# A GAT layer's neighbour differences: made on GpSimd into three buffers instead of on VectorE

## What is computed

```python
h = (x @ W).reshape(G, Jn, H, C)
es = einsum('gjhc,hc->gjh', h, a_s)[:, src]
ed = einsum('gjhc,hc->gjh', h, a_d)[:, dst]
e = leaky_relu(es + ed, 0.2)
alpha = softmax of e over the edges that end in dst
out = zeros.at[:, dst].add(alpha[..., None] * h[:, src]) + bias
x = gelu(layer_norm(out + x @ R, g, b))
```

## Time and profile before

| | us |
|---|---|
| median of 3 runs | 4858.85 (4856.44 to 4862.07) |
| the profiled execution | 4847.68 |
| its span | 4845.9 |
| TensorE busy | 4262.9 (88% of the span) |
| VectorE busy | 3549.6 (73%) |
| ScalarE busy | 2615.6 (54%) |
| GpSimd busy | 627.6 (13%) |
| share of the chain that ended last: TensorE, VectorE, ScalarE, GpSimd | 64%, 18%, 7%, 1% |

### The profile page before, as it was taken

The page is one execution under the profiler, slowest core; times in us unless marked ns, Lnnn a source line. Parts: engine busy times, 40 slices in busy tenths (PEclk is TensorE's granted clock), DMA queues, the critical chain, the costliest instruction groups (busy, mean ns, idle before and its releaser), DMA issues.

```text
span 4845.9 us, 72897 instructions
## 1 busy us (share of the span) xinstructions
PE 4262.9 (88%) x22774; PEld 1939.4 (40%) x22774; DVE 3549.6 (73%) x8027; ACT 2615.6 (54%) x3930; POOL 627.6 (13%) x746
## 2 busy tenths in 40 slices
PE   4687989898998988989988898988899898899988
PEld 4223343443434334343433434344343433434345
DVE  1577777877778877777887777787777887777762
ACT  0454655556565555655555565555555555565643
POOL 1111201111020111102011120111102011110100
PEclk9898999999999999999999999999999999999998
DMA  2000000000000000000000000000000000000000
GB/s 95 2 1 3 1 3 4 2 5 1 3 4 4 4 2 5 1 3 4 3 4 1 6 1 3 4 3 4 1 4 3 4 4 2 5 1 4 3 2 6
DMA packets 23087, 25.64 MB, mean 5 GB/s; under 512 B 3395, under 2 KB 21835, under 8 KB 22139
## 3 DMA queue, kind: packets, MB, share of 16 engines
q1 hardware_dynamic: 22650, 20.26, 1.3%
HBM read 16.06 MB, written 4.19 MB: 4 GB/s over the span
## 4 chain that ended last, share of the span: by engine, by line
PE 64%; DVE 18%; issue 8%; ACT 7%; POOL 1%; DVEq 0%; SPq 0%; DMA 0%; ACTq 0%; POOLq 0%
PE bank L859 11%; PE bank L812 8%; PE bank L925 7%; PE bank L916 6%; PE bank L696 5%; PE bank L829 4%; PE bank L770 3%; PE bank L850 2%; PE bank L815 2%; ACT X L1264 2%; PE bank L708 2%; DVE X L1870 2%; DVE Ho L2019 2%; PE bank L832 1%; PE bank L846 1%
## 5 line engine op out<-in xcount | busy, mean ns | idle before, releaser
L1870 DVE TENSOR_TENSOR X<-X,bank 128x1024 f32<-128x1024 f32 (+2 forms) x432 | 483.7, 1140 | 268.2 <-PE bank L736 153.2
L1264 ACT ACTIVATE X<-X,c_vec 128x1024 f32<-128x1024 f32 (+2 forms) x432 | 498.3, 1176 | 298.3 <-DVE X L1870 297.2
L1308 ACT ACTIVATE X<-bank,bgc 128x512 f32<-128x512 f32 (+1 forms) x624 | 419.2, 672 | 441.9 <-PE bank L859 441.9
L916 PE MATMUL bank<-XT,c_w 128*128 128x512 f32 x1024 | 509.6, 626 | 28.6 <-ACT SQ L1344 26.6
L925 PEld LDWEIGHTS bank<-c_w,SQ 128*128 128x128 f32 x4096 | 481.9, 192 | 56.5 <-issue 50.2
L925 PE MATMUL bank<-c_w,SQ 128*128 128x128 f32 x4096 | 500.8, 277 | 0.0
L812 PE MATMUL bank<-R,c_W 64*128 64x512 f32 (+1 forms) x832 | 473.3, 650 | 28.4 <-issue 23.3
L532 POOL TENSOR_TENSOR R<-X 128x512 f32<-128x512 f32 (+1 forms) x208 | 257.3, 1241 | 1613.4 <-PE bank L812 838.5
L859 PE MATMUL bank<-R,c_C 128*128 128x512 f32 (+1 forms) x832 | 460.2, 635 | 0.0
L846 PE MATMUL bank<-X,WR 64*128 64x512 f32 (+1 forms) x832 | 455.9, 637 | 0.0
L1344 ACT ACTIVATE SQ<-bank,c_vec 128x512 f32<-128x512 f32 x512 | 345.4, 686 | 164.6 <-PE bank L916 162.5
(11 more groups left out here) (258 smaller groups left out, 6822.5 us busy)
## 6 DMA issues: line engine op xcount, KB each, us to landing
c_w<-in_w SPq DMA_DIRECT2D x2, 2048.0 KB
out<-Ho SPq DMA_DIRECT2D x32, 128.0 KB, 2.6
c_fpW<-in_fpW SPq DMA_DIRECT2D x1, 3200.0 KB
X<-in_x SPq DMA_DIRECT2D x34, 75.0 KB, 1.9
X<-in_txt SPq DMA_DIRECT2D x32, 64.0 KB, 1.8
X<-in_chain SPq DMA_DIRECT2D x1, 1300.0 KB
X<-in_sel SPq DMA_DIRECT2D x1, 600.0 KB
X<-in_sel SPq DMA_DIRECT2D x1, 300.0 KB
```

What stands on the lines that cost most here:

```text
L916: mm(hidden_bank(e, m), w1[:, k * P:k * P + P], XT2[:], start=True, stop=True).then_inc(hid_ps, 1)
L1264: A_(dst, dst, ACT.Gelu, bias=v(f"b{l}"), scale=v(f"g{l}")).then_inc(x_ok, 1)
L1308: A_(dst, bZ[k % 2][:, 0:cols], ACT.Identity, bias=bias).then_inc(zs_ok, 1)
L1870: TT(dst, dst, b, ALU.mult).then_inc(u_ok, 1)
```

## The change

`neighbours` of layer 2 loses its difference (two VectorE instructions, one link semaphore and two waits for each chunk) and reads a finished D. A new function `differences_2` on GpSimd makes it, with the same two instructions, into three new buffers `DH` that take the place of the slices of `DR`. It stands in GpSimd's order behind `edges_0` of the next pass and ahead of `pose_pads`. For chunk c it waits for h of chunk c+1 and for VectorE's result of chunk c-2 (which read the buffer). VectorE waits for the new semaphore `dh_ok`; ScalarE's copy of chunk n waits for `dh_ok` of difference n-3, where it waited for VectorE's whole chunk n-3. The constant `LINKS` follows the 13 links that are gone.

```diff
+        DH = [R[:, k * NCOL:(k + 1) * NCOL] for k in (2, 3, 5)]
...
+            def differences_2(s):
+
+                a0 = T0[2] - NT0
+                for c in range(NCH):
+                    n, last_c = joints(c) * P, c == NCH - 1
+                    pool.wait_ge(d_sb, s * AGG + a0 + min(c + 2, NCH))
+                    pool.wait_ge(t_ok, s * AGG + a0 + max(c - 1, 0) + 1)
+                    d, h = DH[c % 3], HS[c % 3]
+                    if last_c:
+                        before_memset(0)
+                        nc.gpsimd.memset(d[:, n - P:n], 0.0)
+                    else:
+                        TT(d[:, n - P:n], HS[(c + 1) % 3][:, 0:P], h[:, n - P:n], ALU.subtract)
+                    TT(d[:, 0:n - P], h[:, P:n], h[:, 0:n - P], ALU.subtract).then_inc(dh_ok, 1)
...
                     edges_0(s + 1)
+                differences_2(s)
+                if nxt:
                     pool.wait_ge(z_ps, s * TASKS + T0[2] + 9)
                     pose_pads(s + 1)
...
-                        act.wait_ge(t_ok, s * AGG + k - 1)
+                        act.wait_ge(dh_ok, s * NCH + n - 2)
...
-            LINKS, LINKS_ANY = 213, 123
+            LINKS, LINKS_ANY = 200, 123
...
                 if l == 2:
-                    dve.wait_ge(t_ok, s * AGG + k + 1)
-                    dve.wait_ge(d_sb, s * AGG + a0 + min(n + 2, NCH))
-                    d, h = DR[:, 0, c % 2, :], HS[c % 3]
-                    if c + 1 < NCH:
-                        TT(d[:, cols - P:cols], HS[(c + 1) % 3][:, 0:P], h[:, cols - P:cols], ALU.subtract)
-                    else:
-                        nc.vector.memset(d[:, cols - P:cols], 0.0)
-                    link(TT(d[:, 0:cols - P], h[:, P:cols], h[:, 0:cols - P], ALU.subtract))
+                    d, before = DH[c % 3], DH[(c - 1) % 3]
+                    dve.wait_ge(dh_ok, s * NCH + n + 1)
                 else:
+                    d, before = DR[:, slot, c % 2, :], DR[:, slot, (c - 1) % 2, :]
                     dve.wait_ge(d_sb, s * AGG + k + 1)
...
-                TT(ta[:, 0:cols], ap[:, 0:cols], DR[:, slot, c % 2, 0:cols], ALU.mult)
+                TT(ta[:, 0:cols], ap[:, 0:cols], d[:, 0:cols], ALU.mult)
```

More of the change, by code:

```diff
@@ L337, in build @@
         dx_ok = sem("dx_ok")
+        dh_ok = sem("dh_ok")
         fp_ps = sem("fp_ps")
@@ L1836, in neighbours @@
                 else:
-                    TT(TB[:, 0:P], am[:, 0:P], DR[:, slot, (c - 1) % 2, NCOL - P:NCOL], ALU.mult)
-                link(TT(TB[:, P:cols], am[:, P:cols], DR[:, slot, c % 2, 0:cols - P], ALU.mult))
+                    TT(TB[:, 0:P], am[:, 0:P], before[:, NCOL - P:NCOL], ALU.mult)
+                link(TT(TB[:, P:cols], am[:, P:cols], d[:, 0:cols - P], ALU.mult))
                 TT(ta[:, 0:cols], ta[:, 0:cols], TB[:, 0:cols], ALU.subtract).then_inc(t_ok, 1)
```

## The result

The changed kernel takes 4868.03 us (median of 20 runs, 4858.72 to 4881.37), the kernel before 4858.55 us on the same chip (20 runs): a ratio of 1.0024, 95% interval 1.0015 to 1.0033. It is slower by 0.24% (9.5 us by the medians), where 10 us less was forecast. Yet the stage that it changes became shorter, by more than forecast.

What follows compares the result with a forecast made beforehand. TensorE bounds the kernel, with holes: 69 us of waits for VectorE in layer 2's stage. Terms: 15 x -0.67 = -10.0 us, about +0.2 in the last pass, giving 4849 us on the runs' median; range 4832 to 4875.

Steps and rivals of the forecast that it cites:

- an earlier end of TensorE's work passes on: Behind layer 2's stage: `rstd` waited 1.10 us for TensorE with VectorE done, so the stage's gain carries through.
- A difference outside this stage: Sign that the forecast is wrong: a change in time anywhere but layer 2's stage; no size given.
- Spread 2 0.93 late: Layer 2's stage, start: L1839 of chunk 0 ends at 622.71 instead of 621.78, so TensorE's spread 2 is 0.93 us late.
- Chunk 2 behind L1591 and L1592, 0.7 late: Layer 2's stage: GpSimd's two instructions take turns with L1591 and L1592 (1.2 us together), making spread 4 0.7 us late.
- Spread 6 0.67 early: Layer 2's stage: chunk 4's L1839 ends at 637.36, so spread 6 comes at 637.42 instead of 638.09, the gain per pass.
- A GpSimd step of 1.42: Layer 2's difference on GpSimd: instructions of 128 and 384 columns, 454 + 1006 ns less some 0.04 overlap, 1.42 us a chunk.
- L1839 slips in between two GpSimd instructions: Chunk 8, layer 2: L1839 runs between GpSimd's small and large instruction, ends at 651.7, and spread 10 is in time.
- rival A: Layer 2's stage: GpSimd keeps the path through both its instructions; gain eaten, +0.3 us a pass, 4863; chance 0.22.
- Rival C, the loop: Layer 2, chunks 7 to 11: the loop over GpSimd becomes the bound, about +2 us a pass, 4889; chance 0.20, half mild.
- The pads hidden: After layer 2's stage: GpSimd's `pose_pads` ends near 662.7, before VectorE wants it, with some 0.5 us of room.
- The last pass +0.2: Layer 2's stage in the last pass, 1.08 us idle before: about 0.2 us longer, small holes absorbing spread 2's 0.9.
- The rule of the Trainium skill: VectorE and GpSimd's shared SBUF path: the first to issue holds it for its whole instruction, the other fully blocks.

Runs made afterwards that it cites:

- a_warm: Changed kernel plus three unread matrix products in two TensorE holes (1.1 and 0.7 us) of layer 0's normalisation: 4835.14 us, 0.9942 of before.
- b_early: Kernel before without layer 2's one-joint difference on VectorE (a stale value is used), nothing new on GpSimd: 4890.72 us, 1.0050 of before.
- a_late: Changed kernel plus two unread products (0.9 us) behind the last sum of layer 2's stage: 4882.05 us, 1.0034 of before.
- a_warm2: Changed kernel plus unread products: three in layer 0's normalisation, three in each of two layer 0 variance holes, three in layer 1: 4823.74 us, 0.9928.
- b_warm2: Kernel before plus unread products in the holes of layer 0's normalisation and variance and ahead of layer 1's third spread: 4837.42 us, 0.9956.

## Why the prediction was wrong

**The stage was right, the sum over the kernel was not.** The step that failed is the sum itself, 15 times the stage's gain, with everything behind the stage taken as unchanged ("an earlier end of TensorE's work passes on"). It passes on for some 65 us behind the stage, to where the changed kernel's clock falls and the other's doesn't. The runs show in its place some 24 us lost outside the stage (the 14 gained and 10 more), with a mean granted clock of 0.954 for 0.959. "A difference outside this stage" stood among the prediction's own signs of being wrong, without a price or a chance. I read TensorE's clock only where the page gives it for the stage (1.00 in the earlier trace rows) and never asked where it falls in a pass, and what a shift does to that. The forecast of -10 us should have carried the clock as a rival of both signs; between kernels whose stages in the second pass are equal to 0.03 us the time differed by some 20 us (4868 and 4891; 4824 and 4843 with the holes filled).

**What the change is worth by itself.** Three pairs with the same filling or shift in both kernels:

| in both kernels | before | changed | ratio of the two ratios to before |
|---|---|---|---|
| three products (warm) | 4845.45 | 4835.14 | 0.9975 |
| more products (warm2) | 4837.42 | 4823.74 | 0.9972 |
| 0.9 us later (late) | 4888.76 | 4882.05 | 0.9977 |
| nothing | 4858.55 | 4868.03 | 1.0024 |

Each of the first three is uncertain by 0.002 to 0.003 and alone hardly tells; together they say -0.25%, some 12 us, which is about what the stage gives (14 us by its lengths, 10 by the forecast), and what the passes of equal clock say (0.85 us each). That the plain pair has the other sign is the case's lesson. That the clock takes the gain is shown by the busy time and clock of the changed kernel, by a_warm and by b_early; how the shift brings on just these stretches is not.

**Point by point.**
- *Spread 2 0.93 late:* 0.87. L1853 of chunk 0 ended 5.94 us behind the stage's start, as worked out (6.0), but not by the way that was worked out:

```profile
617.04 0.69 DVE L1847 TENSOR_TENSOR TA<-bank,R 128x512 f32<-128x512 f32 x1 [4.08 <-POOL R L549]
617.45 1.00 POOL L549 TENSOR_TENSOR R<-R 128x384 f32<-128x384 f32 x1
618.32 0.69 DVE L1853 TENSOR_TENSOR TA<-TA,TB 128x512 f32<-128x512 f32 x1
```

  L1853 kept its 0.69; the sign named was 0.9 to 1.3. VectorE began L1847 0.27 us behind the end of GpSimd's step (616.77), where the sum had 0.15, so L1853 came only 0.13 before GpSimd was done. The whole 0.87 lies in the hand-over (L1847 at 3.97 us from the stage's start for 3.10 before), none in the meeting. That the total fits is in part luck. Of the steps that VectorE waited for, most handed over in 0.28 us. With 0.28 for 0.15 the loop is 6.1 us and its room 0.6, still enough.
- *Chunk 2 behind L1591 and L1592, 0.7 late:* 0.36 (spread 4 at 12.77 us for 12.41). The turns of VectorE and GpSimd took 2.2 us (621.11 to 623.32), not the 2.6 that I had added up. This term was mis-sized, and it is why a pass gained 0.98 and not 0.67.
- *Spread 6 0.67 early:* 0.99, for that reason. The meeting of chunk 4 itself was as worked out: L1853 took 1.02 and ended 0.55 behind GpSimd's end, 20.33 us from the stage's start where I had 20.65:

```profile
631.86 0.99 POOL L549 TENSOR_TENSOR R<-R 128x384 f32<-128x384 f32 x1
632.38 1.02 DVE L1853 TENSOR_TENSOR R<-R,TB 128x512 f32<-128x512 f32 x1
```

- *A GpSimd step of 1.42:* 0.46 and 1.00 with 0.04 to 0.05 overlap, 1.41 to 1.43 undisturbed. Right, from two neighbouring forms.
- *L1839 slips in between two GpSimd instructions (against rival A):* right, and at the chunk of the walk, 8, with GpSimd's step for chunk 9:

```profile
646.72 0.46 POOL L548 TENSOR_TENSOR R<-R 128x128 f32<-128x128 f32 x1 [1.37 <-ACT R L1315]
647.01 0.70 DVE L1853 TENSOR_TENSOR R<-R,TB 128x512 f32<-128x512 f32 x1
647.13 1.45 POOL L549 TENSOR_TENSOR R<-R 128x384 f32<-128x384 f32 x1
```

- *Rival C, the loop:* not the case; from spread 7 on no waits.
- *The pads hidden:* right; GpSimd's last memset ended at 657.83, before VectorE was done with chunk 12.
- *The last pass +0.2:* +0.92. Without the inserted parts nothing gives the start's loss back: spreads 3 and 4 stay 0.5 and 0.9 late. I had let small holes absorb it, but chunk 2 now waits for GpSimd (its L1853 ended at 11.73 us for 10.81), and TensorE sets the pace behind it. That term was mis-sized by 0.7 us, once in the kernel.
- *The rule of the Trainium skill* (SBUF — State Buffer, "Who interferes with whom") held in both orders in the changed kernel: L1853 stretched from 0.69 to 1.02 at chunk 4, L549 from 1.00 to 1.45 beside chunk 8.
- *The time in the range:* 4868 lies in it, but on the side of rivals A and C, neither of which was the cause.

## What to carry to other kernels

A gain of a microsecond in a pass can be smaller than what the shift does to the clock behind it: read the granted clock over a whole pass (and over the whole span of both kernels), at the stretches behind TensorE's holes, before summing a gain over passes. To learn what such a change is worth, measure it twice, once as it is and once with the same fillers in the holes of both kernels; products that nobody reads, in holes that stand anyway, took 15 and 23 us off the kernel before and, by medians of runs at different times, 33 and 44 off the changed one.

## What the runs showed of the hardware

- The granted clock fell to 1.2 GHz in stretches of 3 to some 20 us. The one 112 us behind the stage's start follows two holes of 1.1 and 0.65 us, and three unread products in them kept the clock there at 2.4 GHz (a_warm). Leaving out VectorE's work, as in b_early, cost 30 us, with a mean granted clock of 0.949 for 0.959.
- Passes came in lengths near 283.4, 286.7, 290.1 and 293.2 us, some 3.3 us apart, and hardly between, in the middle passes of both kernels, a_late and a_warm2; a_warm and b_warm2 have lengths between these too (285.7 and 287.5). So in the first four a saving of 1 us a pass is seen as a change in how many passes have which length.
- GpSimd's tensor_tensor of 64 columns took 0.36 us apiece in a row, of 128 columns 0.46, of 384 columns 1.00: cutting one instruction of 384 into six costs 1.15 us.
- A tensor_tensor with both inputs in SBUF, on VectorE, waits for the GpSimd tensor_tensor that runs, and goes ahead of the next one: L1853 beside L549 took 1.02 us for 0.69 and ended 0.55 behind it; L549 that came second took 1.45 for 1.00. Of the GpSimd steps that VectorE waited for, most handed over in 0.28 us (0.27 at 617.04).
